# TensorE products without a reader in the waits at the head of the attention and before the last counts of a two-layer MetaFormer kernel

## The reference

```python
x = x + _L0_conv_ref(_ln_c(x), ...)    # attention-free mixer along the rows
t = t + _L0_ffn_ref(_ln_t(t), ...)     # 8 experts, the best 2 of them, and a shared one
x = x + _L1_conv_ref(_ln_c(x), ...)    # softmax attention inside each image
t = t + _L1_ffn_ref(_ln_t(t), ...)     # 16 experts, the best one, with a capacity
```

```python
q, k, v = x @ Wq, x @ Wk, x @ Wv       # 16, 16 and 128 columns
energy = einsum('bid,bjd->bij', k, q)
attn = softmax(energy, axis=-1)
out = gamma * einsum('bij,bjc->bic', attn, v)
```

## Time and profile before

| what | us |
|---|---|
| median of three runs | 441.15 |
| the three runs | 438.36, 441.15, 447.62 |
| the profiled execution | 442.14 |
| its span, first to last instruction | 440.3 |
| TensorE busy in it | 369.5 (84%) |
| VectorE, ScalarE, GpSimd busy | 298.8, 152.7, 122.9 |

### The profile page before, as it was taken

One profiled execution on the slowest core, in us unless ns is written; L12 is line 12 of the kernel. 1 busy time (PEld: TensorE's weight loads), 2 busy tenths in 40 slices (PEclk: granted clock), 3 DMA queues, 4 the chain that ended last, 5 costly groups with the idle time before them and its releaser, 6 DMA issues.

```text
span 440.3 us, 6484 instructions
## 1 busy us (share of the span) xinstructions
PE 369.5 (84%) x2077; PEld 309.2 (70%) x2077; DVE 298.8 (68%) x943; ACT 152.7 (35%) x323; POOL 122.9 (28%) x140
## 2 busy tenths in 40 slices
PE   5955889869999999888579999997998596998871
PEld 5955889847777777666368999997998462973330
DVE  5846897635665668956564777675765858347997
ACT  3221174363333333233143455763634510331000
POOL 5750140018200000300002570101036673007770
PEclk9999555579999999999855999999899759798987
DMA  8930410035646673230110111110001014852343
GB/s 188 281 118 8 144 69 1 1 85 137 217 148 168 172 229 74 71 74 1 28 37 18 34 35 36 35 24 11 2 19 37 30 49 133 277 195 67 90 115 105
DMA packets 29467, 39.25 MB, mean 89 GB/s; under 512 B 4520, under 2 KB 24809, under 8 KB 29166
## 3 DMA queue, kind: packets, MB, share of 16 engines
q1 hardware_dynamic: 24926, 32.05, 26.8%
q0 software_dynamic: 1728, 3.54, 2.8%
q10 hardware_dynamic: 2784, 3.29, 2.2%
HBM read 22.92 MB, written 12.93 MB: 81 GB/s over the span
## 4 chain that ended last, share of the span: by engine, by line
PE 26%; DVE 14%; POOL 4%; issue 3%; ACT 3%; DMA 1%; SPq 0%; ACTq 0%; DVEq 0%
PE ps L1651 7%; DVE R L1433 6%; POOL slots L1163 3%; PE ps L1744 3%; PE ps L1619 3%; PE ps L1631 2%; PE ps L1699 2%; DVE R L1422 2%; PE ps L1638 1%; PE ps L1763 1%; DVE mx L1244 1%; DVE K L1259 1%; PE ps L1601 1%; PE ps L1600 1%; PE ps L1599 1%
## 5 line engine op out<-in xcount | busy, mean ns | idle before, releaser
L156 POOL TENSOR_TENSOR rstd<-sm,neg_half 128x9 f32<-128x9 f32 x12 | 22.2, 1847 | 195.8 <-DVE sm L150 195.7
L856 PE MATMUL ps<-h,wd 128*128 128x384 f32 x120 | 50.6, 504 | 8.4 <-DVE h L976 7.0
L1651 PE MATMUL ps<-V,wide 128*128 128x129 f32 x400 | 53.5, 284 | 0.0
L831 PE MATMUL ps<-wide,gu_w 128*128 (+1 forms) x108 | 50.8, 471 | 1.6 <-PEq L708 1.6
L923 ACT ACTIVATE s<-ps 128x384 f32<-128x384 f32 (+1 forms) x60 | 29.4, 490 | 61.5 <-PE ps L833 61.1
L1651 PEld LDWEIGHTS ps<-V,wide 128*128 128x128 f32 x400 | 50.3, 199 | 0.0
L971 DVE TENSOR_TENSOR t<-cb,s 128x384 f32<-128x384 f32 x48 | 26.7, 557 | 27.2 <-ACT s L923 19.8
L1433 DVE SCALAR_TENSOR_TENSOR R<-ps,dense_w,R 128x128 f32<-128x128 f32 x144 | 38.0, 342 | 5.8 <-PE ps L1699 5.8
L1244 DVE TENSOR_REDUCE mx<-ps 128x1 f32<-128x576 f32 (+1 forms) x40 | 29.8, 750 | 14.5 <-PE ps L1619 14.4
L1493 ACT ACTIVATE wide<-ps 128x576 f32<-128x576 f32 (+1 forms) x40 | 25.9, 647 | 33.5 <-PE ps L1631 33.5
L832 PE MATMUL ps<-wide,gu_w 128*128 (+1 forms) x108 | 36.4, 337 | 0.0
(11 more groups left out here) (213 smaller groups left out, 797.1 us busy)
## 6 DMA issues: line engine op xcount, KB each, us to landing
cb<-cw SPq DMA_DIRECT2D x24, 384.0 KB, 5.5
slots<-zrow SPq DMA_DIRECT2D x7, 768.0 KB, 7.4
xe<-slots SPq DMA_DIRECT2D x16, 192.0 KB, 3.9
slots<-wide ACTq DMA_DIRECT2D x16, 192.0 KB, 2.8
xall<-in_x SPq DMA_DIRECT2D x8, 288.0 KB, 5.9
out<-R SPq DMA_DIRECT2D x12, 192.0 KB, 2.1
Q<-sQK SPq DMA_DIRECT2D x8, 144.0 KB, 2.4
K<-sQK SPq DMA_DIRECT2D x8, 144.0 KB, 2.5
```

Source lines behind the costliest of these rows:

```text
L831: nc.tensor.matmul(o, gu_w[0][:, w], xTH[:, at], start=True, stop=False)
L856: nc.tensor.matmul(bank[5 + p][:, :CH], wd[:, k, :], h4[q][:], start=k == 0, stop=k == NB2 - 1).then_inc(dn[q], 1)
L1651: last = nc.tensor.matmul(bank[6 + k // 3][:, k % 3 * (C + 1):(k % 3 + 1) * (C + 1)], PT[n % 2][:, jk, i0:i0 + P], V[n % 2][:, jk, :], sta ...
```

## The change

A helper issues products into a bank that is named by the caller. They are 128x384 products in fp32r of the first weights with the first chunk of tokens, and carry no semaphore. It is called in three places on TensorE's queue: three products before each of the energies k = 2, 3, 4 of image 0, fourteen between the row of maxima of image 0 and the transposes of step -1, and eight at the end of step B + 1 = 9, behind the logits of group 2 and before its counts, with a wait on `mL` that its value of B has long reached there.

```diff
+                def keep_clock(times, idle):
+
+                    for _ in range(times):
+                        nc.tensor.matmul(idle[:, :CH], gu_w[0][:, 0:P], hT[:, 0:CH], start=True, stop=True)
+
                 def energies(n, k):
 
+                    if n == 0 and k >= 2:
+                        keep_clock(3, bank[7])
                     if k and n:
                         pe.wait_ge(mx_ok, NB_SS * n + k)
...
                         maxima_row(n + 1)
+                    if n == -1:
+                        keep_clock(14, bank[7])
                     if g is not None:
                         logits(g, 2)
+                    if n == B + 1:
+                        pe.wait_ge(mL, B)
+                        keep_clock(8, bank[2])
                     transposes(n)
```

## The result

The changed kernel takes 442.27 us, the median of 20 runs (439.10 to 444.54). The kernel before, run beside it, takes 441.09 us (20 runs, 435.93 to 447.62). The ratio of the two is 1.006 with a 95% interval of 1.0034 to 1.0086: slower, by 1.5 to 3.8 us. The ratio is of the fast runs, those within 1.5% of each kernel's fastest, which leaves out five runs of the kernel before (444.44 to 447.62 us) and none of the changed one, so it lies above the quotient of the two medians, 1.0027 or +1.2 us. The size, and with it the sign, is so less sure than the interval alone says. Against a bound of 2% it is no change.

A forecast was written before the change was run, and what follows sets the result against it. Chain in n = 0 passes through TensorE only in pieces between ScalarE and VectorE, later through GpSimd's scatters; 0.1 + 0.4 + 0 + 0.1 + 0 = +0.6 us on 441.15 us gives 441.8 us, range 437 to 446 us.

The forecast's parts named there:

- the first rival: The clock holds through n = 0 and n = 1: -4.4 us, so 436.8 us; chance 0.15.
- (A): Nine products before energies k = 2, 3, 4 of image 0: taken +0.1 us, ends -0.3 and +0.8 us.
- (B): Fourteen between the maxima and the next transposes: they eat what the higher clock gives, +0.1 to +0.7, taken +0.4 us.
- (C): Rest of n = 0: the clock falls again before the V products; taken 0, ends -2.4 if it holds, and 0.
- (D): n = 1: the clock rises where it rose before; taken +0.1 us, ends -2.1 and +2 us.
- (E): Eight before the counts of group 2: hidden by a 3.16 us wait; taken 0, ends 0 and +1.4 us.
- the rise at 222.5 us: Sign at the head: the granted clock rises between 219 and 223 us.
- the fourteen 0.18 us apart: Sign behind the maxima of image 0: the fourteen products start about 0.17 us apart.
- the Q and K products: Sign in n = 0: their end lies 5.8 to 6.4 us behind the start of the maxima.
- the fall: Sign in n = 0: the clock falls again near 230 us.
- the scatters: Sign at the second place: GpSimd's scatters keep their 1.29 us.

The follow-up runs named there:

- the tail only: Changed kernel with only the eight products before the counts of group 2, no nine or fourteen: 439.91 us, ratio 1.0021 to the kernel before.
- the head only: Changed kernel without the eight before the counts, keeping the nine and the fourteen: 442.29 us, ratio 1.0072 to the kernel before.
- step 0 only: Kernel before plus only twelve and two products before energies k = 2 and k = 3 of image 1: 472.18 us, ratio 0.9971.
- the twenty-eight: Changed kernel with twenty-eight products in place of the fourteen and none before the counts: 477.82 us, ratio 1.0063 to the kernel before.
- nine and step 0: Kernel before plus the nine, and twelve and two before energies k = 2, 3 of image 1: 469.06 us, ratio 0.9870; again 467.26 us, 0.9823.
- the fourteen and step 0 filled: Changed kernel without the eight, plus twelve and two products before energies k = 2, 3 of image 1: 470.94 us, ratio 0.9926 to the kernel before.

## Why the prediction was right, and where it was off

**The forecast.** 441.8 us and a range of 437.0 to 446.0 us, with "no change at 2%" at 0.95; measured 442.27 us. As a difference the sum was +0.6 us. The medians say +1.2 us, the ratio +1.5 to +3.8 us: right in sign, and too small by 0.6 us or by 1 to 3 us. The working has one slip: it gives the first rival as -4.3 us once and -4.4 us in its sum, and -4.4 us is what the terms give.

**The pair of traces agrees with +0.6 us by luck.** From the first Q and K product of the first image (L887) to the maxima of image 2 it takes 46.07 us before (206.46 to 252.53) and 46.62 us after (207.10 to 253.72), +0.55 us. But that is the sum of +0.97 us ahead of the nine, where the clock was lost already at 212.3 us and not at 216.1 us, +0.45 us for the nine, +0.55 us in step 0 and -1.42 us in step 1. The first and the last are differences between executions. Without products at the head (the tail only) the same stretch takes 44.52 us, with the head only 46.59 us. So the traces put the change at +0.5 to +2.1 us.

**(A), the nine: a value at the low side.** Taken as +0.1 us, with ends -0.3 and +0.8. What they can change lies between the start of the Q and K products ahead of them (L1587, 215.90 us before) and the maxima (222.24 us). Where the clock was down at that start, the stretch takes 6.52 us without the nine, in both such traces (the fourteen only, step 0 only); with them it takes 6.79 us in the changed kernel, 7.39 us with the head only, and 6.32 to 6.97 us in three more: -0.2 to +0.9 us. Where the clock fell less than 1 us behind that start, it takes 6.34 us (before) and 5.85 us (the tail only) without, and 6.08 to 6.10 us with them, in three traces. In the two traces dearest of all, with the head only and with the twenty-eight, six to nine of them were issued at 0.32 us before the clock rose. The value taken lies inside what was found; in the changed kernel's own two traces the nine cost +0.3 and +0.9 us, so it was too small for them.

**(B), the fourteen: right, and so is its reason.** The end of the Q and K products was to lie 5.8 to 6.4 us behind the maxima; it lies 230.55 - 224.30 = 6.25 us behind, +0.54 us where I took +0.4. The energies behind the next wait start 9.18 us after the maxima in place of 8.63 us, +0.55 us:

```profile
233.48 0.85 PE L1626 MATMUL ps<-Q,K 97*128 97x288 f32 x2 [2.19 <-DVE mx L1244]
```

```profile
230.87 0.85 PE L1619 MATMUL ps<-Q,K 97*128 97x288 f32 x2 [1.97 <-DVE mx L1244]
```

With nine and step 0 the same distance is 7.32 us, with the fourteen and step 0 filled 9.18 us. So the raised clock gives 1.31 us here and the fourteen take 1.86 us: they eat what the clock gives, as the working says.

**(C), step 0: right.** The clock fell at 232.7 us, predicted for 230 to 233, and the V products ran at 1.2 GHz. From the energies behind the wait to the next maxima it takes 7.23 us before and 7.23 us after: the term is 0. In the runs with filled waits it takes 4.8 us, 2.4 us less, which is the end that the prediction gave if the clock holds. In the 10.2 us of raised clock TensorE was busy 7.18 us, and the fall came in the wait of 2.19 us behind the last Q and K products. With the nine alone and with the twenty-eight it came 1.1 and 0.5 us behind the end of that wait. Products in it held the clock, or raised it, in all seven traces that have them.

The Trainium skill (TensorE: Matmul & The Clock Gate, "HAM oscillation") was weighed there: waits between bursts drop the clock anew. The trace agrees: the clock fell at 232.7 us, in a wait of 2.19 us. The Trainium skill (TensorE: Matmul & The Clock Gate, Part 1) says of a ramp that its penalty is "<1% of a typical kernel span". Here the low stretch at the head, of 24 to 27 us, was worth 4.8 to 5.8 us of two steps with its waits filled and the fourteen left out, 1.1 to 1.3% of 441 us. The figure is of one ramp and this of a whole low stretch, so it shows only that such a stretch can be worth more than one ramp.

**(D), step 1: not the change.** Taken +0.1; 13.01 us against 14.43 is -1.4 us, but 13.35 and 13.37 us in two other traces, one of which has nothing changed at the head. So it depends on where the rise falls in an execution.

**(E), the eight: right.** Hidden in the wait, beside a chain of GpSimd; the tail alone is at 1.0021 with 1 in its interval.

**The signs.** Of those that the prediction names, the rise at 222.5 us, the fourteen 0.18 us apart, the Q and K products, the fall and the scatters came as said. Step 0 with 16.41 us lies 0.1 us above the 15.5 to 16.3 us, and step 1 with 13.01 us well below the 14.4 us.

**What is left open.** The traces give +0.5 to +2.1 us, the medians +1.2 us; the ratio's interval begins at 1.5 us, and nothing here shows where anything beyond 2.1 us would be spent. With the nine ahead of them the fourteen were never seen to begin at 1.2 GHz, so the 2.45 us which that costs in step 0 (18.31 against 15.86) cannot be claimed for it. How the times split over executions with an early and a late fall, the runs don't show.

## What to carry to other kernels

Products without a reader held the clock where they stood in the wait in which it was lost. Ahead of work that others wait for they cost TensorE's time for them, 0.17 to 0.18 us each at 2.4 GHz and 0.32 us at 1.2 GHz, less only what a wait there hides (0.7 of 2.5 us here). Look for the fall, not for the low stretch: raise the clock just before the dense work, fill the longest wait behind it, and leave out the rest. Before any of it, ask from the chain whether TensorE sets the pace there: at the scatters the eight changed nothing that could be measured, and in the feed-forward waits neither did a clock of 1.00.

## What I had not expected of the hardware

The kernel before took 439 us on one chip and 475 us, twice, on another; the traces there have steps of the attention of the same length. The surplus sits in waits in the last third, among them those that the profile gives to "another core or an unknown queue" (3.55, 5.70 and 8.73 us in one trace), and I can't name their cause.

Unbroken work did not raise the clock everywhere. In the kernel before, TensorE was busy for the whole of these 5.04 us at 0.50, and the rise came at 243.4 us only:

```profile
232.56:237.60 5.04, 5.04 (x23) 0.50 0.00 0
```

The clock's path is not the same twice: it rose for good in the feed-forward part at 91.4 to 105.4 us, fell between 211.9 and 218.4 us in the thirteen of fourteen traces that lose it there, and had short low stretches at other places in each. Two executions of one kernel can so differ by more than the 0.6% that were to be found; the length of one named step, read in each, was a better witness than the span.
